# A cross-network kernel: who adds the two halves of layer 0's accumulator copy

## The reference, cut to what matters

```python
h = inputs                                   # (512, 40, 32)
for i, (W, bias) in enumerate(params):       # 3 layers of 200 maps
    x = jnp.einsum('bhd,bmd->bhmd', h, inputs).reshape(B, -1, D)
    y = jax.nn.relu(jnp.einsum('oi,bid->bod', W, x) + bias[None, :, None])
    if i != n_layers - 1:
        h, direct = jnp.split(y, 2, axis=1)  # 100 maps go on, 100 go out
    else:
        direct = y
    outs.append(direct)
result = jnp.concatenate(outs, axis=1).sum(-1)
...
h = jnp.maximum(h @ W_top1 + b_top1, 0.0)    # then W_top2, W_top3
```

## Time and profile before

| | us |
|---|---|
| median of 3 runs | 2819.57 (2819.26 to 2823.86) |
| the profiled execution, whole | 2822.93 |
| its span, first to last instruction | 2821.1 |
| TensorE busy | 2775.4 (98%) |
| VectorE busy | 2637.9 (94%) |
| ScalarE busy | 1500.6 (53%) |
| GpSimd busy | 858.7 (30%) |
| mean granted TensorE clock | 0.998 |

### The profile page before, as it was taken

One profiled execution on the slowest core, in us unless ns is written; L12 is line 12 of the kernel. 1 busy time (PEld: TensorE's weight loads), 2 busy tenths in 40 slices (PEclk: granted clock), 3 DMA queues, 4 the chain that ended last, 5 costly groups with the idle time before them and its releaser, 6 DMA issues.

```text
span 2821.1 us, 54038 instructions
## 1 busy us (share of the span) xinstructions
PE 2775.4 (98%) x19012; PEld 2758.2 (98%) x19012; DVE 2637.9 (94%) x1945; ACT 1500.6 (53%) x1880; POOL 858.7 (30%) x700
## 2 busy tenths in 40 slices
PE   5999999999999999999999999999999999999999
PEld 4999999999999999999999999999999999999997
DVE  6999999999999999999999999999999999999995
ACT  4555555555555555555555555555555555555553
POOL 5433332332332332332323323323323323333100
PEclk9999999999999999999999999999999999999999
DMA  7333333433433433333334334334333334334330
GB/s 210 85 83 84 86 94 78 94 87 76 99 88 75 100 84 82 97 84 85 93 79 94 87 78 97 89 75 102 85 78 99 85 82 95 85 86 94 85 78 18
DMA packets 286025, 249.66 MB, mean 89 GB/s; under 512 B 31286, under 2 KB 284446, under 8 KB 285893
## 3 DMA queue, kind: packets, MB, share of 16 engines
q1 hardware_dynamic: 216310, 200.56, 25.4%
q0 software_dynamic: 65712, 45.56, 12.1%
q10 hardware_dynamic: 3972, 3.17, 0.4%
HBM read 140.74 MB, written 4.20 MB: 51 GB/s over the span
## 4 chain that ended last, share of the span: by engine, by line
PE 94%; POOL 2%; DVE 1%; DMA 1%; issue 1%; SPq 0%; ACT 0%; another core or an unknown queue 0%; DVEq 0%; ACTq 0%; POOLq 0%
PE acc L809 62%; PE acc L811 29%; POOL gathered L445 1%; PE z_ps L826 1%; PE hid_ps L822 1%; DVE tails L721 1%; DMA acc_copy<-acc_copy 1%; DVE product L716 1%; PE acc L880 0%; SPq L380 0%; DMA gathered<-in_table,rows_all 0%; PE hid_ps L903 0%; DMA hid_rep<-hid 0%; ACT acc_copy L528 0%
## 5 line engine op out<-in xcount | busy, mean ns | idle before, releaser
L809 PE MATMUL acc<-weights,heads 126*128 126x400 f32 (+1 forms) x9088 | 2694.1, 364 | 16.3 <-DVE tails L721 16.2
L811 PE MATMUL acc<-weights,tails 126*128 126x200 f32 (+1 forms) x9088 | 2321.6, 255 | 0.0
L522 ACT ACTIVATE heads<-product 126x1024 fp32r<-126x1024 f32 (+2 forms) x1152 | 1198.1, 1047 | 1021.5 <-PE acc L811 507.3
L811 PEld LDWEIGHTS acc<-weights,tails 126*128 126x128 f32 (+1 forms) x9088 | 1740.8, 192 | 0.0
L809 PEld LDWEIGHTS acc<-weights,heads 126*128 126x128 f32 (+1 forms) x9088 | 1712.9, 188 | 19.7 <-issue 10.0
L721 DVE TENSOR_TENSOR tails<-product,heads 126x1024 fp32r<-126x1024 f32 (+2 forms) x1152 | 1348.9, 1204 | 1.4 <-ACT heads L522 1.1
L716 DVE TENSOR_TENSOR product<-hid_rep,x_rep 126x2048 f32<-126x2048 f32 x510 | 1167.4, 2289 | 96.5 <-PE acc L811 64.8
L453 POOL DMA_DIRECT2D acc_copy<-acc_copy x189 | 235.0, 1244 | 1719.8 <-ACT acc_copy L528 1716.4
L445 POOL DMA_INDIRECT gathered<-in_table,rows_all x320 | 510.8, 1596 | 101.4 <-issue 97.1
L536 ACT ACTIVATE y_relu<-acc_copy 128x400 f32<-128x400 f32 x192 | 102.4, 533 | 217.0 <-DMA acc_copy<-acc_copy 215.0
L528 ACT ACTIVATE acc_copy<-acc 128x800 f32<-128x800 f32 x192 | 158.7, 827 | 9.8 <-PE acc L811 7.7
(11 more groups left out here) (26 smaller groups left out, 118.2 us busy)
## 6 DMA issues: line engine op xcount, KB each, us to landing
x_rep<-x_rows SPq DMA_DIRECT2D x512, 120.0 KB
hid_rep<-hid SPq DMA_DIRECT2D x511, 120.0 KB
x_pairs<-x_rows SPq DMA_DIRECT2D x191, 280.0 KB
acc_copy<-acc_copy POOLq DMA_DIRECT2D x189, 200.0 KB
hid_rep<-hid SPq DMA_DIRECT2D x511, 5.0 KB
x_pairs<-x_rows SPq DMA_DIRECT2D x63, 120.0 KB
gathered<-in_table,rows_all POOLq DMA_INDIRECT x320
raw_weights<-in_w SPq DMA_DIRECT2D x8, 500.0 KB, 6.1
```

Of the source, the lines that this page charges most:

```text
L522: act.activation(heads[0:rows, ring % HEADS_RING, 0:tiles, :], product[0:rows, ring % PRODUCT_RING, 0:tiles, :], ACT.Copy).then_inc(heads_ ...
L809: nc.tensor.matmul(acc[:, at.parity, c, 0:2 * LAYER], dims(heads[0:rows, ring % HEADS_RING, k, :], c), w, start=(q == 0 and k == 0), stop= ...
L811: last = nc.tensor.matmul(acc[:, at.parity, c, LAYER:2 * LAYER], dims(tails[0:rows, ring % PRODUCT_RING, k, :], c), w[:, 0:LAYER], start=F ...
```

## The change

`vector_slots` now holds the layer 0 slot of every block, beside the two that it held of the last layers 1 and 2. GpSimd's `add` skips these, so 63 more slots lose their accumulating DMA. VectorE calls `sum_halves` for layer 0 right after the product of the groups 4 and 5 of the layer that follows layer 0 in the iteration. `relu` waits for `halves_summed` in every layer 0, and counts the fewer DMAs of the others.

```diff
-        vector_slots = [place(0, 0).slot, place(1, blocks - 1).slot, place(2, blocks - 1).slot]
+        vector_slots = [place(0, b).slot for b in range(blocks)] + [place(1, blocks - 1).slot, place(2, blocks - 1).slot]
...
             def relu(layer, at, b):
-                if at.slot in vector_slots if isinstance(at.slot, int) else False:
-                    act.wait_ge(halves_summed, vector_slots.index(at.slot) + 1)
+                if layer == 0:
+                    act.wait_ge(halves_summed, b + 1)
+                elif isinstance(b, int) and b == blocks - 1:
+                    act.wait_ge(halves_summed, blocks + layer)
+                elif isinstance(b, int):
+                    by_dma = [s for s in range(at.slot + 1) if s not in vector_slots]
+                    act.wait_ge(y_summed, 16 * len(by_dma))
                 else:
-                    act.wait_ge(y_summed, (at.slot - (isinstance(at.slot, int) and at.slot > vector_slots[1])) * 16)
+                    act.wait_ge(y_summed, (b + layer) * 32 - 16 * (3 - layer))
...
                         make_products(layer, at, q, i - layer, parity)
+                        if l0 and first and layer == first[0] and q == 4:
+                            sum_halves(*l0)
                         if last_turn and q == 4:
                             fold(*first)
```

## The result

| | before | after |
|---|---|---|
| median, us | 2819.69 (4 runs) | 2926.62 (4 runs, 2918.54 to 2930.78) |
| profiled span, us | 2821.1 | 2928.8 |
| mean granted TensorE clock | 0.998 | 0.992 |

The change makes the kernel slower: ratio 1.0375, 95% interval 1.0361 to 1.0389. The forecast was 2911 with a range of 2887 to 2941. The profiled execution is the longest of the four after the change and has the lowest granted clock: the others took 2918.5, 2924.0 and 2929.3 us at 0.996, 0.994 and 0.994.

A forecast was written before the change was run, and what follows sets the result against it. TensorE was taken as the bound: 60 blocks at 1.5 us make 90, plus 1.5 for blocks 1 to 3; 91.5 on the profiled 2822.9 gives 2914.4, less 3.4 for the median: 2911 us, range 2887 to 2941.

The forecast's parts named there:

- The bound: TensorE, busy 98% of the span, bounds the kernel; any delay that reaches it is paid in full.
- What goes is worth nothing: GpSimd's 63 removed DMAs, 78 us of a mostly idle engine, and the earlier stores save 0.
- VectorE's work fits by busy time: VectorE's sum adds 0.5 us to a block of 42.9 us in which it is idle 2.0.
- The chain: Layer 2's DMA, relu, layer 0's copy, sum, tails 2: TensorE's group 2 starts 1.42 us late on average.
- c: End of layer 0's copy on ScalarE, counted from the start of layer 0's matmuls; mean taken as 8.43 us.
- The restart: TensorE's matmuls resuming at group 2 after the wait cost 0.09 us more.
- it just fits: At group 4 the delayed tails end at 1425.91, TensorE wants them at 1425.99: no second loss.
- step 5: The block shown loses 1.65 us; VectorE's later work moves by 2.15 us, yet group 4 has no second loss.
- The DMA lands later: Rival, 10%: stores right behind layer 2's DMA delay its landing 0.5 us a block, 30 us more, 2941.
- The clock: Rival, 7%: TensorE's clock falls after waits, 1.8 us each; 3021 us if after all 60, 2939 if one in four.
- The page's figure: Skill's estimate of 2.5 us for layer 2's DMA, making the sum cost 0; set aside for the traced 4.6 us.

The follow-up runs named there:

- the DMAs left out: The change without VectorE's layer 0 sums in blocks 1 to 63, so nobody adds those halves and the 63 DMAs stay removed: 2821.3 us, ratio 1.0001.
- the first experiment: Kernel before, with VectorE adding 400 numbers a partition of a spare tile at the sum's place, without waiting: 2827.4 us, ratio 1.0021.
- the sum behind tails 3: The change, with the sum moved behind the tails of group 3, about 9.5 us after layer 0's start: 2827.5 us, ratio 1.0017.
- between tails 4 and 5: The change, with the sum moved between the tails of groups 4 and 5: 2824.9 us, ratio 1.0010; run once more, 2822.7 us, ratio 1.0011.
- Wait and work: Kernel before, with VectorE waiting for layer 0's copy and then adding 400 numbers of a spare tile, GpSimd's DMAs kept: 2913.6 us, ratio 1.0332.
- stores as before: The change, with GpSimd waiting for layer 0's copy before the two stores: 2919.2 us, ratio 1.0357.

## Why the prediction was right, point by point

- **The bound.** TensorE was the bound, and a delay reached it in full: right. It is now idle for 91 us ahead of L816, where 80 had been forecast, in 65 waits, where about 60 had.
- **What goes is worth nothing.** Right: ratio 1.0001 with the DMAs left out.
- **VectorE's work fits by busy time.** Nearly right: alone it costs 0.2%, since at group 4 the tails then end only 0.10 us ahead. Its busy time rose by 36 us where 30 had been put, as each sum counts with its whole 0.58 us.
- **The chain.** Right step by step. VectorE's wait was 1.49 us in the block shown; the sum started 0.03 us behind the copy, the tails 0.49 behind that, TensorE 0.06 behind their end. Late by 1.42 was forecast on average, with c at 8.43, and c came out at 8.46.
- **The restart and "it just fits".** What a delay costs beyond its length came to 0.15 us where 0.09 had been put, 3.5 us over 59 blocks. The restart itself was right: within group 2 the matmuls fall behind by 0.09 to 0.10. The other 0.04 to 0.05 are lost at group 4, where step 5 had found room: its tails end 0.10 us ahead, near the 0.08 of that step, and the first matmul takes 0.41 us instead of 0.36. That so small a lead costs time had been put at nothing; the first experiment and the sum behind tails 3 show the same loss without any wait, and between tails 4 and 5 it is gone.
- **The DMA lands later.** The mean of c rose by 0.05 us over all profiles with early stores, in place of the 0.5 of the rival, but a sixth to a third of the copies end late where it was at most a twelfth. That the mean of the kernel before, 8.43, came so near the change's 8.46 is in part luck.
- **The clock** had been given 7% as a case that applies to a quarter of the blocks or to all, at 1.8 us each, and the forecast had it at nothing. In the profiled execution it applied to six of 59 periods at 1.5 us each, 9.2 us. This is the largest part of the 16 us by which the forecast was low; the start-up (5.5 us where 1.5 had been put) is the next. From 30 us to block 4 the mean granted clock was 0.92 after and 0.95 before, which may be its cause; no run tried it. All of it lies inside the range.
- **The page's figure.** Of the landing of layer 2's DMA, 707.69 to 712.19 in the block shown, this trace gives 4.5 us. The Trainium skill, "DMA: Bandwidth & Descriptors", section "Anatomy of one DMA — SWDGE (gpsimd) path", puts such a DMA at 2.0 us and its bytes at 436 GB/s, an estimate of 2.5 us, by which nothing would have been lost. The measured figure decides.

## What to carry to other kernels

A step that is moved to a busy engine costs little by its own length and much by what it must wait for: find the end of the chain that feeds it, and put it behind the last instruction that someone else needs before then. Here the same sum costs 0.1% instead of 3.75% when it stands 6 us further down VectorE's order. Before a wait is taken away, see whether the waiting engine ever came early enough to feel it. And where TensorE is the bound, the price of an idle stretch rises faster than its length, because the clock can fall behind it: 1.3 us of idle a block cost 0.16 us of clock a block in the change's profile, and 3.4 us cost 1.8.

## What the runs showed of the hardware

- A fall of TensorE's clock can follow rather short idle time, and not surely. In the change's 59 steady periods, 11 waits of 1.67 to 2.39 us of counted idle had six falls behind them, and 48 shorter ones had none. Wait and work, and stores as before, had only three waits of that length between them (2.16, 2.17 and 2.02 us), and none was followed by a fall. With waits of 3.4 us on average the fall came in 58 of 59 periods; the one without had the shortest wait, 2.85 us. What decides in a single case was not settled.
- A matmul stream can lose time that no view counts as idle: 0.05 us a block in the first experiment, seen in the period, in the count of matmuls in 400 us, and in a first matmul of 0.41 us where the stream has 0.36. It happened where the tails ended 0.10 us ahead of their matmul, and not where they ended 0.16 us ahead.
- In the change the sum is followed by the next instruction 0.49 us after its own start, though it shows 0.58 us: what it adds to a full VectorE is less than its duration by about 0.09 us.
